# A post-norm decoder layer on one core: attention outputs turned by VectorE, and self attention's full-array products put ahead of its small ones

## The chip, the core and the metric

One core of a Trainium2 chip. Its engines are TensorE (PE, with a weight-load queue PEld), VectorE (DVE), ScalarE (ACT), GpSimd (POOL) and SyncE (SP, which here only issues DMAs). The metric is the device time of one execution in microseconds (us), as the median of several.

## What is computed

The input x has 8 batches of 512 tokens of width 256, and a context has 1024 tokens for each batch. Three sub-layers follow each other, each with the post-norm form x = layernorm(x + f(x)).

```
# self attention, 16 heads, key size 64, value size 16
scores = einsum(Q, K) / 8
Wmat   = scores * decay(t, s) * lam[level(t, s)]        # level: size class of t XOR s, 10 used
o      = einsum(Wmat, V) @ Wout.T + x;  layernorm(o) * ln_g + ln_b
# cross attention, 16 heads of size 16, 1024 keys
out    = softmax(q k / 4) v @ Wo.T + bo
# experts: 32 experts choose 8 tokens of each batch
probs  = softmax over tokens of (x @ gate_w.T + gate_b), then top_k(8)
merged = the chosen tokens weighted;  o = w2 gelu(w1 merged);  scatter-add o * vals
```

## The kernel before

The kernel is one program with three blocks, written out engine by engine. Every engine has its own instruction stream, and semaphores order the streams. In each stream the order is that of the code; nothing is scheduled by a tool. A block starts when every engine has left the one ahead of it.

**Self attention** (`self_attention`) runs through 8 batches of 8 head pairs, in sections `first`, `mid`, `last` and a `tail`. In iteration `i` TensorE works on three pairs at once: it projects queries and keys of pair i (`project_qk`, L468, 128x128 weights), makes the near scores of pair i-1 (`scores`, L501, tiles of 64x32) and its keys by token (`keys_by_token`, L490, transposes with 128x128 weights), and finishes pair i-2 (`states` L481, tiles of 128x64; `far` L516 and L522, tiles of 64x64; `near` L531, tiles of 32x32). PSUM results go through two lanes: `psA` with two slots, emptied by ScalarE, and `psV` with two slots, emptied by VectorE. `take_a` and `take_v` wait for the slot's last content to be gone. In the tail the first projections of cross attention run between the last pairs, and the layer norms of the last batch: GpSimd's `add_lnb` and `scale_by_lng` (L920, L914), VectorE's split of the projected keys in bf16 parts (`parts`, L183 to L192), whose rows the DMAs of `stack` (L200, L201) put into place.

**Cross attention** (`cross_attention`) first does 12 positions of maxima alone, and then 32 steps for each of 8 batches: 4 groups ("quads") of 4 heads, by 8 chunks of 128 keys. A step has the scores S of its chunk (L1459), four score products for the maxima of the step 12 ahead (`max_scores`, L1398), which VectorE reduces (L1680) from the three slots of `cpsV`, and the values product of the step before (`values`, L1420, four column tiles that add up in `acc`, called cacc in the trace). ScalarE takes the exponentials (L1586). Between these, at fixed steps, stand the jobs of the batch before (`prev`) and of the next one (`nxt`).

The path from `acc` to the output projection is what the change touches. After each quad ScalarE copies `acc` to `OT` (L1616); TensorE transposes it in four parts (`o_transposes`, L1439) in the step behind, ahead of the values product; VectorE divides by the sums (`outputs`, L1708, L1712) into O. When four quads are done TensorE transposes O in 8 parts (L1360 at step 2), ScalarE copies the result to oT (L1558), and at step 4 TensorE projects it (L1475) in four groups, each in a slot of `cpsV`. Later the gate's logits come from 4 recorded products with 32 columns of weights and 512 tokens (L1482, step 12), each streaming 512 columns; VectorE adds a bias (L1754), looks for the 8 largest and masks them; at step 20 the probabilities P8 are ready and SP saves them (L1319).

**SP's queue** issues in program order. In step 20 and behind it the order is: the save of P8, 12 DMAs of `stack_later(b + 1, 1)`, then `stack_max(b, 3)` (L1286), which moves the maxima nmT (12 KB) to where S of step 24 needs them. In the last batch weights of the experts are loaded by the same queue (`load_group_weights`, L1165, 1 MB each): 4 MB ahead of `stack_max(b, 3)`, and 8 MB at the end of the last step.

**Experts**: 8 groups of 4 experts, 8 MB of weights each group, loaded when the buffers come free; the loads of the fourth group's weights wait for the first group's first product and are issued after some small loads of SP.

Of the kernel before, what the change touches and what calls it, by code (L numbers as in the profile page):

```python
# [25 lines left out]
P = 128  # L26
# [5 lines left out]
G = T // P  # L32
# [103 lines left out]
OUTPUTS, X1T, PROJECT_V1, PROJECT_Q, MERGE, PROJECT_O, NORM = 1, 0, 1, 4, 2, 4, 7  # L136
PROJECT_K, X2T, COPY_X2, GATE, GATE_EXP, TOP8, TOP8_T, PICK, PICK_T = (7, 12), 9, 10, 12, 14, 20, 21, 28, 29
PROJECT_V0 = 20
# [173 lines left out]
def self_attention(nc, sh, dram):  # L312
    with ExitStack() as ctx:
# [103 lines left out]
        def _(pe):  # L417
            def body(sec, b):
# [194 lines left out]
                for i in range(PAIRS if now else 4):  # L613
# [13 lines left out]
                    if opening:  # L627
                        transpose_distances()
                        scored = take_v(("score", i))
# [7 lines left out]
                    if now:  # L637
                        project_qk(qk, 1, i)
                    if i == 2 and prev:
                        transpose_y()  # L640
                    if two is not None:
# [44 lines left out]
        def _(act):  # L686
            def body(sec, b):
# [71 lines left out]
                for i in range(PAIRS):  # L759
# [39 lines left out]
                    if sec == "tail" and i == 6:  # L799
# [3 lines left out]
                        nc.scalar.copy(ca.Vc[:, :, 0:8, 0:HD], full("cv").rearrange("p (c h d) -> p c h d", c=KT, d=HD)  # L803
# [7 lines left out]
        def _(pool):  # L811
# [19 lines left out]
            def body(sec, b):  # L831
# [69 lines left out]
                def layer_norm_factors(r):  # L901
                    pool.wait_ge(var, b * 2 + (r - 1))
# [38 lines left out]
                for i in range(PAIRS):  # L941
# [10 lines left out]
                    if i == 4 and prev:  # L952
                        add_lnb()
# [4 lines left out]
                    if i == 5 and prev:  # L958
                        scale_by_lng()
                    if i == 7 and prev:  # L960
                        layer_norm_factors(1)
                    if i == 1 and sec == "tail":
# [4 lines left out]
                        nc.gpsimd.memset(ca.Vc[:, :, :, HD:HD + 1], 1.0).then_inc(ca.vc_zeroed, 1)  # L967
# [7 lines left out]
        def _(dve):  # L975
# [3 lines left out]
            def body(sec, b):  # L979
# [117 lines left out]
                for i in range(PAIRS):  # L1097
# [37 lines left out]
                    if i == 6 and prev:  # L1135
                        dve.wait_ge(lnb_added, b)
                        dve.wait_ge(n1_scaled, b)
# [39 lines left out]
def ca_jobs(section):  # L1177
# [9 lines left out]
    for s in range(STEPS if now else TAIL_STEPS):  # L1187
# [3 lines left out]
        if prev:  # L1191
            a += {MERGE: ["oT"], X2T: ["x2T"]}.get(s, [])
# [6 lines left out]
        if s % KT == OUTPUTS and (now and s > KT or prev and s < KT):  # L1199
            v.append(("otr", (s // KT - 1) % QUADS))  # L1200
        if prev:
            v += [("wo", g) for g in range(G) if s == PROJECT_O]
# [921 lines left out]
```

## Time and profile before

| | us |
|---|---|
| median of 3 runs | 1839.48 |
| the three runs | 1838.58, 1839.82, 1839.48 |
| the profiled execution | 1839.74 |
| its span | 1837.9 |
| granted clock, mean over the span | 0.953 of full speed |

| stage | from, to (us of the span) |
|---|---|
| self attention, from the first products to its last pair | 22 to 594 |
| hand-over to cross attention | 594 to 629 |
| maxima alone | 629 to 660 |
| 8 x 32 steps of cross attention | 660 to 1646 |
| tail of cross attention for the last batch | 1646 to 1676 |
| experts, combine and store | 1676 to 1838 |

The profiled execution is 1.8 us longer than its span. Stage borders are read from the first and last instruction of each on TensorE. In rows of the timeline an entry merges equal instructions in a row; the distance from one row's start to the next one's is the time that the first took in the queue, which is less than its duration, since matmuls overlap at their ends. A matmul in float32 is recorded twice, a transpose once.

### The profile page before, as it was taken

The page shows a single profiled execution, that of the slowest core. Times are in us where ns is not written, and L with a number is a line of the kernel's source. Part 1 is how long each engine was busy: PE and PEld are TensorE (multiplying, and loading weights), DVE is VectorE, ACT ScalarE, POOL GpSimd, SP SyncE. Part 2 cuts the span into 40 slices and gives each one's busy share as a digit, 9 for nine tenths or more (in the row PEclk, how much of TensorE's full clock was granted, in tenths as well). Part 3 has the DMA queues.
Part 4 walks back from the last instruction along what each step waited for, and adds up shares of the span by engine and source line. Part 5 has one row for each costly group of instructions (what it writes and reads, how often), then busy time and mean ns, then how long its engine had stood idle before and what let it go on. Part 6 is the DMA issues. An engine that isn't in the chain of part 4 may idle for free. (4 is left out here: it accounts for less than half of the span.)

```text
span 1837.9 us, 48963 instructions
## 1 busy us (share of the span) xinstructions
PE 1678.5 (91%) x19924; PEld 806.8 (44%) x19924; DVE 1232.9 (67%) x2424; ACT 838.3 (46%) x1015; POOL 598.2 (33%) x970
## 2 busy tenths in 40 slices
PE   5999999999999699999999999999999999976564
PEld 3566666666665333343333433433433334223332
DVE  5767677677674777868778788788687787812005
ACT  2334344344333136655646565566556465651103
POOL 3545545645625536043043061250430420000002
PEclk8999999999999779999999999999999999987777
DMA  7000000000000221111202101112112024046995
GB/s 252 3 4 4 3 3 3 3 3 3 3 32 15 69 67 50 41 38 59 83 1 85 56 28 65 50 38 69 35 64 78 1 89 183 30 179 267 421 418 183
DMA packets 62205, 141.44 MB, mean 77 GB/s; under 512 B 11280, under 2 KB 34320, under 8 KB 54320
## 3 DMA queue, kind: packets, MB, share of 16 engines
q1 hardware_dynamic: 61520, 137.88, 20.6%
q8 instruction: 157, 2.57, 0.6%
q10 hardware_dynamic: 480, 0.59, 0.1%
q14 instruction: 48, 0.39, 0.1%
HBM read 92.43 MB, written 7.86 MB: 55 GB/s over the span
## 5 line engine op out<-in xcount | busy, mean ns | idle before, releaser
L1680 DVE TENSOR_REDUCE mx<-cpsV 128x1 f32<-128x512 f32 x1024 | 655.2, 686 | 187.5 <-PE cpsV L1398 175.3
L1586 ACT ACTIVATE w<-cpsA 128x1024 f32<-128x1024 f32 x512 | 496.3, 1021 | 246.0 <-PE cpsA L1459 240.8
L1398 PE MATMUL cpsV<-w 96*128 96x512 bf16 x1024 | 325.4, 394 | 21.6 <-DVEq L1663 13.0
L1459 PE MATMUL cpsA<-w 99*128 99x512 bf16 x1024 | 275.2, 382 | 22.4 <-DMA w<-nmT 10.1
L1420 PE MATMUL cacc<-w 128*32 128x512 f32 x2048 | 279.7, 607 | 0.4 <-ACT w L1586 0.4
L468 PE MATMUL psA<-w 128*128 128x512 f32 x512 | 257.0, 625 | 5.0 <-DVE WT L1102 1.8
L1398 PEld LDWEIGHTS cpsV<-w 96*128 96x128 bf16 x1024 | 86.1, 98 | 283.4 <-DVE mx L1680 197.0
L1648 POOL TENSOR_TENSOR crstd<-cmv,eps 128x4 f32<-128x4 f32 x8 | 1.6, 202 | 605.8 <-DVE cmv L1746 605.8
L765 ACT COPY w<-psA 128x1024 f32<-128x1024 f32 x64 | 64.8, 1012 | 229.3 <-PE psA L468 229.3
L1459 PEld LDWEIGHTS cpsA<-w 99*128 99x128 bf16 x1024 | 93.0, 98 | 163.0 <-ACT w L1564 15.8
L885 POOL TENSOR_TENSOR VP<-V,VPF 128x128 f32<-128x128 f32 (+2 forms) x256 | 129.2, 535 | 42.7 <-PE psA L481 36.8
L1111 DVE TENSOR_TENSOR tmp<-psV,CF 128x512 f32<-128x512 f32 x64 | 44.3, 692 | 121.7 <-PE psV L531 121.4
L468 PEld LDWEIGHTS psA<-w 128*128 128x128 f32 x512 | 87.9, 191 | 76.5 <-issue 67.7
L183 POOL TENSOR_TENSOR w<-w,zero 128x256 bf16<-128x256 f32 x88 | 51.1, 612 | 138.8 <-ACTq L1565 138.8
L1420 PEld LDWEIGHTS cacc<-w 128*32 128x32 f32 x2048 | 42.5, 108 | 92.5 <-issue 74.5
L2031 DVE TENSOR_TENSOR z<-psE,b1T 128x256 f32<-128x256 f32 x8 | 3.4, 424 | 110.5 <-PE psE L1967 110.5
L1981 PE MATMUL psE<-w,hT 128*32 128x256 f32 x512 | 39.6, 477 | 36.5 <-DMA w<-in_w 34.6
L1564 ACT COPY w<-cpsA 128x1024 f32<-128x1024 f32 x21 | 21.3, 1012 | 111.5 <-PE cpsA L1368 59.9
L1118 DVE TENSOR_REDUCE w<-tmp 128x128 f32<-128x512 f32 x64 | 67.8, 1059 | 4.7
L501 PEld LDWEIGHTS psV<-w 64*32 64x32 f32 x4096 | 41.2, 106 | 49.8 <-issue 48.1
L1385 PEld LDWEIGHTS cpsA<-w,w 128*128 128x128 f32 x480 | 54.7, 192 | 12.6 <-ACT w L1586 12.6
L192 POOL TENSOR_TENSOR w<-w 128x256 bf16<-128x256 f32 x88 | 57.1, 680 | 3.1
(224 smaller groups left out, 2227.6 us busy)
## 6 DMA issues: line engine op xcount, KB each, us to landing
w<-in_w SPq DMA_DIRECT2D x56, 1024.0 KB, 16.3
w<-w SPq DMA_DIRECT2D x189, 128.0 KB, 2.3
w<-w SPq DMA_DIRECT2D x189, 64.0 KB, 2.0
w<-in_ctxT SPq DMA_DIRECT2D x8, 1024.0 KB, 5.0
w<-in_xT SPq DMA_DIRECT2D x8, 512.0 KB, 6.4
x_tok<-in_x SPq DMA_DIRECT2D x8, 512.0 KB, 9.7
w<-in_w SPq DMA_DIRECT2D x8, 512.0 KB, 17.2
out_y<-w SPq DMA_DIRECT2D x16, 256.0 KB, 2.3
```

Source lines behind the costliest of these rows:

```text
L183: ops.tensor_tensor(cut(high, m), cut(r, m), zeros, ALU.add)
L192: ops.tensor_tensor(cut(low, m), cut(r, m), cut(mid, m), ALU.subtract)
L468: last = nc.tensor.matmul(out[:, n * T:(n + 1) * T], w[:, k, i * P:(i + 1) * P], XT[:, b, k, :], start=(k == 0), stop=(k == KD - 1))
L765: nc.scalar.copy(QK[:, i % 4, :], full(("qk", i))).then_inc(act_evac, 1)
L885: last = nc.gpsimd.tensor_tensor(VP[:, p % 2, g, 0:n, :].rearrange("q n (h c) -> q n h c", c=HD), vv.unsqueeze(1).broadcast_to([P, n, 2, HD]),
L1118: nc.vector.tensor_reduce(yp, tmp[:].rearrange("p g s c -> p g c s"), AX_X, ALU.add)
L1385: last = nc.tensor.matmul(out[:, c * P:(c + 1) * P], cT[:, k, c * P:(c + 1) * P], wv[:, k, hv * P:(hv + 1) * P], start=(k == 0), stop=(k = ...
L1398: nc.tensor.matmul(out, Qst[q // 2][0:ROWS, hh, g * P:(g + 1) * P], Kst[q // 2][0:ROWS, hh, half * BANK:(half + 1) * BANK], start=True, st ...
L1420: last = nc.tensor.matmul(acc[BLK * jj:BLK * (jj + 1), :], Vc[:, chunk, 4 * q + jj, :], Pr[:, (2 * s + jj // 2) % 4, (jj % 2) * T:(jj % 2 ...
L1459: last = nc.tensor.matmul(out[:, n * T:(n + 1) * T], Kst[q // 2][0:ROWS + 3, hh, chunk * P:(chunk + 1) * P], Qst[q // 2][0:ROWS + 3, hh, : ...
L1586: nc.scalar.activation(Pr[:, (2 * s + pp) % 4, :], src, ACT.Exp, scale=CA_SCALE).then_inc(act_evac, 1)
L1680: nc.vector.tensor_reduce(mx[:, q % 2, row, k % 2:k % 2 + 1], full(m[k]), AX_X, ALU.max).then_inc(dve_evac, 1)
```

## The change

Self attention: in an iteration TensorE now does queries, keys and keys by token in a row, and behind them scores, far and near. In the tail `add_lnb` is done ahead of the first norm's factors, and the product with ln_g by VectorE instead of GpSimd.

Cross attention: VectorE takes `acc` itself (`take_outputs`: a transpose in blocks of 32x32 from PSUM), divides, and transposes back (`outputs`); a DMA (`move_o`) puts 64 rows of each quad into oT. ScalarE's copy, both sets of TensorE's transposes and the copy to oT are gone. The values stand interleaved with zeros in Vc. The output projection has two groups of twice the width; the gate's logits come from column tiles, four token groups side by side, and four DMAs put them in one row block (`L4` to `L`), a step earlier than before; x2T goes in two jobs. In the tail `keep_clock` issues transposes of the identity that nothing reads.

```diff
@@ TensorE, self attention, iteration i
-                    if one is not None and not opening:
-                        scored = take_v(("score", i))
-                        evacuated_a(before(i, "qk"))
                     if now:
                         qk = take_a(("qk", i))
                         project_qk(qk, 0, i)
-                    if one is not None:
-                        scores(scored, one)
-                    if two is not None:
-                        out = take_v(("far", i))
-                        evacuated_a(("state", i))
-                    if now:
                         project_qk(qk, 1, i)
                     if i == 2 and prev:
                         transpose_y()
+                    if one is not None:
+                        evacuated_a(before(i, "qk"))
+                        keys_by_token(i, one)
+                        scores(take_v(("score", i)), one)
                     if two is not None:
+                        out = take_v(("far", i))
+                        evacuated_a(("state", i))
                         far(out, two)
...
-                    if one is not None:
-                        keys_by_token(i, one)
-                    if two is not None:
                         near(out, two)
@@ SP, cross attention
+            def move_o(bb, q):
+                sp.wait_ge(o_ready, bb * QUADS + q + 1)
+                sp.dma_start(oT[64 * (q % 2):64 * (q % 2) + 64, q // 2, :], byd[q % 2][0:P:2]
+                             ).then_inc(o_moved[q % 2], 16)
@@ TensorE, cross attention
-                    if s % KT == OUTPUTS and (now and s > KT or prev and s < KT):
-                        o_transposes(b if s > KT else b - 1, (s // KT - 1) % QUADS)
+                    if sec == "tail" and s == 1:
+                        pe.wait_ge(acc_evac, b * QUADS + 1)
+                        keep_clock(34)
                     if prev:
                         if s == PROJECT_O:
-                            evacuated_a("oT")
-                            for g in range(G):
-                                out = take_v(("wo", g))
...
+                            for of in o_moved:
+                                pe.wait_ge(of, b * 32 + 16)
+                            for r in range(2):
+                                out = take_v(("wo", r))
...
+                            keep_clock(28)
                         if s == GATE:
                             out = take_v("lg")
-                            evacuated_a("x2T")
+                            evacuated_a(("x2T", 1))
                             for k in range(KD):
-                                last = nc.tensor.matmul(out[0:E, :], gw[:, k, :], x2T[:, k, :],
-                                                        start=(k == 0), stop=(k == KD - 1))
+                                for g in range(G):
+                                    last = nc.tensor.matmul(out[E * g:E * (g + 1), 0:P], gw[:, k, :],
+                                                            x2T[:, k, g * P:(g + 1) * P], start=(k == 0), stop=(k == KD - 1))
                             last.then_inc(dve_full, 1)
+                            keep_clock(52)
...
-                    if prev and s == MERGE:
-                        pe.wait_ge(o_ready, b * QUADS)
-                        transpose_x("oT", O)
@@ VectorE, cross attention
+                def take_outputs(bb, q):
+                    dve.wait_ge(av_done, (bb * QUADS + q + 1) * KT)
+                    nc.vector.transpose(byq[q % 2][:].rearrange("p c s -> p (c s)"), acc[:]).then_inc(acc_evac, 1)
                     dve.drain()
+                def outputs(bb, q):
+                    t = byq[q % 2]
+                    nc.vector.reciprocal(rec[:], t[:, :, 1])
+                    dve.drain()
+                    nc.vector.tensor_tensor(t[:, :, 0:BLK:2], t[:, :, 0:BLK:2], rec[:].unsqueeze(2).broadcast_to([P, KT * 2, HD]),
+                                            ALU.mult)
+                    dve.drain()
+                    dve.wait_ge(o_moved[q % 2], bb * 32 + (q // 2 + 1) * 16)
+                    nc.vector.transpose(byd[q % 2][:], t[:].rearrange("p c s -> p (c s)")).then_inc(o_ready, 1)
+                    dve.drain()
...
+                    if now and s == TOP8:
+                        outputs(b, 1)
...
+                    if now and s and s % KT == 0:
+                        take_outputs(b, s // KT - 1)
+                    if prev and s == 0:
+                        take_outputs(b - 1, 3)
```

`outputs` stands at step 12 for quad 0 (behind a wait for the moved logits), at step 20 for quad 1 (behind P8), and at step 1 of the next batch for quads 2 and 3. In the last batch quad 2 is done at step 27.

TensorE in self attention, one iteration in the middle of a batch, first before and then after (psV and psA are the two lanes; w is a weight buffer):

```order
L481 MATMUL psA<-VP,Kt 64x48 x2
L468 MATMUL psA<-w_0 128x512 x2
L501 MATMUL psV<-w_1 32x32 x32
L468 MATMUL psA<-w_0 128x512 x2
L516 MATMUL psV<-Mst,w_1 64x64 x12
L516 MATMUL psV<-Mst,w_1 64x48 x4
L522 MATMUL psV<-Mst,w_1 64x16 x4
L490 MATMUL psA<-ident,w_1 128x128 x4
L531 MATMUL psV<-V,WT 32x16 x32
```

```order
L481 MATMUL psA<-VP,Kt 64x48 x2
L468 MATMUL psA<-w_0 128x512 x4
L490 MATMUL psA<-ident,w_1 128x128 x4
L501 MATMUL psV<-w_1 32x32 x32
L516 MATMUL psV<-Mst,w_1 64x64 x12
L516 MATMUL psV<-Mst,w_1 64x48 x4
L522 MATMUL psV<-Mst,w_1 64x16 x4
L531 MATMUL psV<-V,WT 32x16 x32
```

The three stretches with full 128x128 weights became one, and the three small products stand behind each other.

VectorE in cross attention around the end of a quad, before and after (mx<-cpsV are the maxima, 4 a step):

```order
L1680 TENSOR_REDUCE mx<-cpsV 128x1 x18
L1708 RECIPROCAL rec<-cpsV 128x16
L1712 TENSOR_TENSOR O<-cpsV,rec 128x64 x4
L1680 TENSOR_REDUCE mx<-cpsV 128x1 x10
L1685 TENSOR_REDUCE nm<-mx 128x16
```

```order
L1704 TENSOR_REDUCE mx<-cpsV 128x1 x16
L1732 STREAM_TRANSPOSE byq<-cacc 128x512
L1704 TENSOR_REDUCE mx<-cpsV 128x1 x12
L1709 TENSOR_REDUCE nm<-mx 128x16
```

The take now stands right behind the maxima of the quad's last step, two maxima sooner than the old division.

SP's queue at the end of cross attention, before and after (w_0 and w_1 from in_w are the experts' weights, byd is what `outputs` leaves):

```order
L1165 DMA w_0<-in_w 128x2048 x4
L1286 DMA w_1<-nmT 3x16x128
L1165 DMA w_1<-in_w 128x2048 x8
L1319 DMA p_scratch<-P 32x512
L1221 UNCONDITIONAL_BRANCH
```

```order
L1164 DMA w_0<-in_w 128x2048 x4
L1287 DMA w_1<-nmT 3x16x128
L1293 DMA oT<-byd 64x512
L1164 DMA w_1<-in_w 128x2048 x8
L1293 DMA oT<-byd 64x512
L1323 DMA L<-L 32x128 x4
L1339 DMA p_scratch<-P 32x512
L1218 UNCONDITIONAL_BRANCH
```

Behind the last eight loads of weights there is now a move of the last quad's outputs, and then the four of the logits.

## Rows read from the trace of the kernel before

**Rows 1.** Busy time by stage: PE, PEld, DVE, ACT, POOL, clock, DMA share, GB/s.

```profile
60.00:572.00 512.00, 507.16 (x12391) 328.09 (x12389) 349.94 (x640) 192.04 (x284) 259.58 (x418) 1.00 0.02 6
660.00:1644.00 984.00, 950.05 (x5264) 362.93 (x5262) 747.03 (x1509) 572.78 (x615) 244.94 (x398) 0.99 0.18 60
```

**Rows 2.** Timeline of TensorE, one pair: start, duration, line, operation, count.

```profile
304.16 0.76 PE L501 MATMUL psV<-w 64*32 64x32 f32 x64
304.85 1.98 PE L468 MATMUL psA<-w 128*128 128x512 f32 x4
306.76 0.68 PE L516 MATMUL psV<-Mst,w 64*64 64x64 f32 x32
...
307.46 0.66 PE L490 MATMUL psA<-ident,w 128*128 128x128 f32 x4
308.05 0.73 PE L531 MATMUL psV<-V,WT 32*32 32x16 f32 x64
308.79 0.79 PE L481 MATMUL psA<-VP,Kt 128*64 128x64 f32 x20
```

**Rows 3.** Timeline of the weight loads in the same pair.

```profile
302.78 0.19 PEld L468 LDWEIGHTS psA<-w 128*128 128x128 f32 x1 [0.24 <-issue]
303.21 0.19 PEld L468 LDWEIGHTS psA<-w 128*128 128x128 f32 x1 [0.24 <-issue]
```

**Rows 4.** Timeline, hand-over to cross attention.

```profile
610.03 1.22 DVE L183 TENSOR_TENSOR w<-w,zero 128x1024 bf16<-128x1024 f32 x1 [0.95 <-ACTq L746]
...
612.63 3.39 DVE L189 TENSOR_TENSOR w<-w,zero 128x1024 bf16<-128x1024 f32 x1
...
616.09 3.21 DVE L192 TENSOR_TENSOR w<-w 128x1024 bf16<-128x1024 f32 x1
```

**Rows 5.** Timeline of TensorE, steps 8 and 9 of a batch.

```profile
946.66 0.61 PE L1398 MATMUL cpsV<-w 96*128 96x512 bf16 x2
...
948.43 0.66 PE L1439 MATMUL cpsV<-ident,OT 128*128 128x128 f32 x4
949.02 1.06 PE L1420 MATMUL cacc<-w 128*32 128x512 f32 x8
950.01 1.09 PE L1522 MATMUL cpsA<-ident,o 128*128 128x128 f32 x8
950.94 0.60 PE L1398 MATMUL cpsV<-w 96*128 96x512 bf16 x2
```

**Rows 6.** Timeline of VectorE at the same place.

```profile
947.09 2.59 DVE L1680 TENSOR_REDUCE mx<-cpsV 128x1 f32<-128x512 f32 x4 [0.24 <-PE cpsV L1398]
```

**Rows 7.** Instructions of line L1047: count, ns (least, median, most).

```profile
L1047 DVE STREAM_TRANSPOSE w<-w x16: 1245/1245/1246, 52.2 to 545.3; 128x1024 f32<-128x1024 f32 x16
```

**Rows 8.** Timeline of TensorE, output projection at step 4.

```profile
923.52 2.86 PE L1475 MATMUL cpsV<-cwo,oT 128*128 128x256 f32 x12 [0.55 <-DVE mx L1680]
```

**Rows 9.** Timeline of SP and TensorE ahead of step 24.

```profile
874.08 0.77 SPq L1286 DMA_DIRECT2D w<-nmT  x1
...
876.33 1.04 PE L1459 MATMUL cpsA<-w 99*128 99x512 bf16 x4 [0.18 <-DMA w<-nmT]
```

**Rows 10.** The same step in the last batch.

```profile
1615.62 0.73 SPq L1286 DMA_DIRECT2D w<-nmT  x1
...
1625.11 1.89 PE L1459 MATMUL cpsA<-w 99*128 99x512 bf16 x4 [7.45 <-DMA w<-nmT]
```

**Rows 11.** Timeline of the tail: SP's weights, the projection, the next weights.

```profile
1643.21 4.27 SPq L1165 DMA_DIRECT2D w<-in_w  x8
...
1650.49 6.26 PE L1475 MATMUL cpsV<-cwo,oT 128*128 128x256 f32 x16 [1.10 <-ACT oT L1558]
...
1682.47 36.49 SPq L1165 DMA_DIRECT2D w<-in_w  x24
```

**Rows 12.** Stretches of the tail and of the experts, columns as in rows 1.

```profile
1660.00:1665.00 5.00, 3.27 (x10) 1.93 (x11) 1.36 (x4) 1.96 (x2) 0.00 (x0) 0.50 0.95 397
...
1677.00:1800.00 123.00, 84.33 (x928) 43.13 (x931) 3.82 (x9) 15.32 (x24) 2.54 (x9) 0.82 0.99 403
```

More of the change, by code:

```diff
@@ L901, in layer_norm_factors @@
                 def layer_norm_factors(r):
+                    if sec == "tail" and r == 0:
+                        pool.wait_ge(dve_evac, SA_DVE.count(sec, b, ("out", 1)) + DVE_SLOTS)
+                        add_lnb()
                     pool.wait_ge(var, b * 2 + (r - 1))
@@ L951, in body @@
                         level_logits()
-                    if i == 4 and prev:
+                    if i == 4 and prev and sec != "tail":
                         add_lnb()
@@ L1191, in ca_jobs @@
         if prev:
-            a += {MERGE: ["oT"], X2T: ["x2T"]}.get(s, [])
+            a += [("x2T", k) for k in range(KD) if s == X2T]
         if nxt:
@@ L1240, in cross_attention @@
         nmT = sb("nmT", [48, P], BF16)
-        OT = sb("OT", [P, T])
-        rec = sb("rec", [P, G, 4])
-        O = sb("O", [P, G, D])
+        byq = [sb(f"byq_{n}", [P, KT * 2, BLK]) for n in range(2)]
+        byd = [sb(f"byd_{n}", [P, T]) for n in range(2)]
+        rec = sb("rec", [P, KT * 2])
         o2 = sb("o2", [P, G, D])
@@ L1296, in body @@
                     stack_later(b, 3, free=CA_ACT.count(sec, b, ("s", 0, 1)) if prev else None)
+                if prev:
+                    if sec != "tail":
+                        move_o(b - 1, 2)
+                    move_o(b - 1, 3)
+                if now:
                     sp.wait_ge(act_full, CA_ACT.count(sec, b, ("v", 1)))
@@ L1433, in v0_evacuated, with keep_clock @@
                     return CA_ACT.start["mid"] + (b - 1) * CA_ACT.per_batch - back + 1 + 2
-                def o_transposes(bb, q):
-                    out = take_v(("otr", q))
-                    pe.wait_ge(acc_evac, bb * QUADS + q + 2)
-                    for g in range(G):
-                        last = nc.tensor.transpose(out[:, g * P:(g + 1) * P], OT[:, g * P:(g + 1) * P], sh.ident[:])
-                    last.then_inc(dve_full, 1)
+                def keep_clock(count):
+                    if sec == "tail":
+                        for _ in range(count):
+                            nc.tensor.transpose(acc[:, 0:P], sh.ident[:], sh.ident[:])
                 if sec == "pro":
@@ L1590, in body @@
                     if prev:
-                        if s == MERGE:
-                            to_rows("oT", oT)
                         if s == X2T:
-                            to_rows("x2T", x2T)
+                            for k in range(KD):
+                                nc.scalar.copy(x2T[:, k, :], full(("x2T", k))[:, 0:T]).then_inc(act_evac, 1)
                         if s == COPY_X2 and sec != "mid":
@@ L1611, in body @@
                             evac_v(0)
-                    if s % KT == 0 and ((now and s) or (prev and s == 0)):
-                        bb, q = (b, s // KT - 1) if s else (b - 1, 3)
-                        act.wait_ge(av_done, (bb * QUADS + q + 1) * KT)
-                        nc.scalar.copy(OT[:], acc[:]).then_inc(acc_evac, 1)
             sections(act, body)
@@ L1727, in body @@
                         max_jobs(s + LEAD, 0, 1)
-                    if s % KT == OUTPUTS and (now and s > KT or prev and s < KT):
-                        outputs((s // KT - 1) % QUADS)
+                    if prev and s == 1:
+                        if sec != "tail":
+                            outputs(b - 1, 2)
+                        outputs(b - 1, 3)
                     if prev:
@@ L1780, in body @@
                                                   ).then_inc(dve_evac, 1)
+                    if sec == "first" and s == GATE_MAX:
+                        outputs(b, 0)
+                    if now and s == TOP8:
+                        outputs(b, 1)
+                    if sec == "last" and s == LAST_OUTPUTS:
+                        outputs(b, 2)
                     if maxima:
```

126 lines of the change are left out of this document (71 added, 55 removed).

## The prediction

> **What bounds the kernel now.** I read the stretches by stage first, then the timeline of TensorE in each stage, then the waits where it stood idle. [rows 1] is the whole story of two thirds of the time: in self attention TensorE is busy for 507.16 of 512 us, in the steps of cross attention for 950.05 of 984, at full clock. VectorE follows with 747 of 984. So what counts is what stands in TensorE's queue, and what makes it stop. In the tail and the experts it is another matter: TensorE is half idle, and from 1677 to 1800 the DMAs are the bound, and the end moves with the moment at which the next weights are issued (rows in the part on the tail).
>
> **Self attention: three stretches of full weights become one.** [rows 2] is one pair in TensorE's queue, and [rows 3] gives the pace of a 128x512 product when nothing changes: two weight loads are 0.43 apart. Four of them, the keys, would take 1.72, but stand 306.76 - 304.85 = 1.91 in the queue: 0.19 is lost where small tiles follow. The queries lose as much ahead of the scores. The transposes by token take 308.05 - 307.46 = 0.59 for four; by [rows 5] eight take 950.94 - 950.01 = 0.93, so a transpose costs about 0.11 and four 0.43: 0.16 lost. Three such ends are 0.54, one is left: 0.38 a pair is gained. What comes in: scores ahead of far, and far ahead of near, two changes between small forms. The trace has one such change, near to states: 0.74 in the queue for 64 products with 0.63 of loads, 0.11. Two of them are 0.22. They replace two changes from small to full, of which 64 scores show one: 0.69 in the queue for the same loads, so 0.06 to 0.07; two are 0.14. Net 0.08 against: **0.30 a pair**, 62 pairs with all three parts, 18.6 us. Bounds: the new changes free, 0.52 a pair (32 us), or as dear as those after full products, 0.19 each, 0.14 a pair (9 us).
>
> Here a rule speaks: the Trainium skill, "TensorEngine Tiling (Array Packing)", section Key Properties, says that a change of tiling mode drains TensorE, and makes no difference between modes. An iteration had 7 changes and will have 5. At one price for all, 0.19 from [rows 2], two fewer give 0.38 a pair, 23.6 us and a total of 1819. The trace shows the changes to be unequal, dear after full products and cheap after small ones, so I stay with the sum by rows.
>
> New waits there: keys by token now need their slot of psA right behind Y's transposes (i = 2), while ScalarE still empties keys and queries (1.01 for 1024 columns, against 0.93 of transposes and some latency): 0.2 for 7 batches, 1.4 us. The other slots have more than an iteration's small products as cover (some 2.1 us), VectorE keeps its own distance: far's results are asked for 5.2 us after near has ended.
>
> **Hand-over: 4.2 us.** The split in parts takes 1.22 an operation when GpSimd is quiet, but 3.39 and 3.21 while it adds lnb and multiplies by lng [rows 4]. Everything to the start of cross attention hangs behind (copy, stacking DMAs, last norm). With add_lnb ahead and the product on VectorE behind the split, both fall to 1.22: 4.2 us.
>
> **Cross attention, quads.** Removed: four transposes ahead of the values, 949.02 - 948.43 = 0.59 each quad [rows 5]. Added: VectorE must have taken acc before the next values may start. The maxima of the quad's last step are issued at 946.66; VectorE works on them from 947.09, two in half of 2.59 [rows 6], to 948.39. A transpose of 128x1024 takes 1.245 [rows 7]; for 512 I estimate 0.7 (half is 0.62, a reduction of 512 from PSUM takes 0.65). So acc is free at 949.1, and TensorE, a semaphore later, starts the values at 949.18 instead of 948.43: it stands for 0.75. A quad loses 0.16 net; 31 quads, 5 us. The old division hid between maxima; the new one (reciprocal, product, transpose, about 1.6) stands at step 1 (twice), 12 and 20, where 3.5 us of V or K projection follow and leave VectorE idle. Without that cover it would cost its whole length.
>
> **Per batch.** O's eight transposes go, 0.93 [rows 5], and a wait for their copy, 0.24. The projection waits 0.55 and a little more for slots [rows 8]; with two slots wanted instead of four that is gone: 0.9. The gate's four products are streamed in 4 x 0.43 = 1.7 [rows 3]; four token groups side by side need a quarter, 0.45: 1.25 gained. x2T in two jobs: 0.15. Sum 3.45 a batch. The detour of the logits by DMA (issue four times 0.4, landing 2.2) is over when VectorE comes to it at step 12, about.
>
> **SP's queue.** At step 20 `move_o(b, 1)` comes ahead of the 12 stacking DMAs and waits until VectorE has done P8 *and* the outputs. The maxima's move lands 876.33 - 874.08 = 2.25 after issue, and S of step 24 waits for it already, 0.18 in this batch [rows 9]. It comes later by 1.6 for the outputs, plus the move's issue, less the save that used to run meanwhile: 1.75. Queued behind S on TensorE is all else. I take 1.65 for six middle batches, 9.9 us lost.
>
> Together: 7 batches x 3.45 = 24 would be gained, but in the last one what is gained ahead of step 8 only meets the maxima's move behind 8 MB of weights, and step 24 shifts by 1.75 [rows 10]: 6 x 3.45 = 20.7 and nothing for the last. 20.7 - 5 - 9.9 = **5.8 us** gained.
>
> **The tail: a loss.** Before, the last outputs reach the projection by ScalarE and TensorE at 1650.49 [rows 11]. Now they go by a DMA that SP issues at about 1648, behind eight loads of 1 MB. What a small transfer does behind large ones is in [rows 10]: 12 KB issued at 1615.62, behind 4 MB, landed at 1625.1, 9.5 instead of 2.25 later, and TensorE stood for 7.45. The 8.4 MB need 20 us at 0.42 MB a us; the stretch 1660 to 1665 is still 0.95 busy [rows 12]. So the projection starts at 1664.7, **14.2 us late**. `keep_clock(34)` fills 3.6 us of that and the rest is idle.
>
> Behind it things are faster. The granted clock there is 0.50 in 1660 to 1665 [rows 12], so products take double. The gate goes from 4 x 0.86 (twice the 0.43) to 0.5, the projection has one stall less, the copy of x2T overlaps, the fillers hold the clock for the small transposes; against that the logits' DMAs take 3.5. Step by step I come to P8T's end 2.7 earlier, counted from the projection. Net 11.5 us, and the reload of weights, and with it the end, moves by that: the next weights are issued at 1682.47 [rows 11], and from then to 1800 the DMA share is 0.99 [rows 12].
>
> A rule speaks against the fillers: the Trainium skill, "TensorE: Matmul & The Clock Gate", Part 4, has it that transposes don't count as work for the clock. By it the fillers do nothing, about 2 us more. No row of before shows whether transposes alone keep it up.
>
> **Sum**, against the profiled 1839.74: -18.6 + 1.4 - 4.2 - 5.8 + 11.5 = -15.7, so 1824.0; the median of the runs is 0.3 below the profiled one: **1823.8**.
>
> **Rivals.**
> *The small transfer overtakes the weights.* For it: a transfer is spread over 16 engines and is small. Against: [rows 10]. Then it lands 2.25 after 1648, at 1650.4, and the tail is 2.7 shorter instead of 11.5 longer: 1809.6.
> *Changes between small forms cost more than those after full products.* One mechanism, in TensorE's self attention. Each 0.01 of a change is 62 x 0.02 = 1.24 us. From 0.26 a change on the whole is slower (15 x 1.24 = 18.6 us away from the 0.11 taken); at 0.30 it is 24 more, 1847. For it: no row shows scores ahead of far, or far ahead of near, and the split of the array changes at each. Against it: near to states, 0.11.
> *VectorE becomes the bound in cross attention.* It is 76% busy in [rows 1] and gets 2.3 instead of 1.4 a quad; if the divisions aren't covered, 31 x 1.6 = 50 more, 1873; it loses all gain when 0.5 of each shows. For it: it idles only some 0.24 between two maxima. Against: the places, each in a projection's shadow.
> *The fillers don't hold the clock*: 1825.8, and nothing else changes.
>
> **Chances.** Forecast, with the fillers' case (a tenth) inside: 0.70. Overtaking 0.10. Small changes dear 0.12. VectorE bound 0.08. The forecast's own range comes from the bounds: small changes free or 0.19 each (-14, +10), take of acc 0.62 to 0.9 (-3, +6), SP's delay 0 to 1.75 a batch (-10, +1), tail by 3 each way. I give 1808 to 1841, which takes in the overtaking case. Under 0.2% (3.7 us) is no change that a measurement can tell. Faster 0.82, same 0.06, slower 0.12.
>
> **What would show it.** In the timeline after: in a pair, queries to the end of near 0.3 shorter, with no gap at far; S to values at a quad's end with TensorE waiting 0.75 for byq (L1732); S of step 24 waiting about 2 for nmT in the middle batches; a landing of the last move at 1645 + 19 on the old scale, with the projection waiting for it; the split's operations 1.22 each. Wrong: if the projection in the tail waits for VectorE and not for a DMA; if TensorE waits for a division; if the pair has the old length.

## The result and the profile after

| | us |
|---|---|
| before, median of 4 runs on the same chip | 1839.65 |
| after, median of 4 runs (1882.34 to 1888.22) | 1885.41 |
| ratio, with its 95% interval | 1.0249 (1.0231 to 1.0267) |
| forecast | 1823.8 |

The change made the kernel 46 us slower where 16 us of gain were forecast. Landmarks on TensorE, GpSimd and SP cut both spans into the same four pieces, which shows at once where to look:

| piece | before | after | difference | forecast |
|---|---|---|---|---|
| start to the first maxima (self attention and hand-over) | 628.89 | 658.16 | +29.3 | -21.4 |
| first maxima to the last values product | 1015.6 | 1015.7 | 0.0 | -5.8 |
| last values to the next weights issued by SP | 37.9 | 55.3 | +17.3 | +11.5 |
| from there to the end | 155.4 | 155.6 | +0.2 | 0 |

In the first piece the hand-over did as foretold. The split's operations in the timeline of VectorE, after, against [rows 4]:

```profile
643.43 1.23 DVE L183 TENSOR_TENSOR w<-w,zero 128x1024 bf16<-128x1024 f32 x1 [0.96 <-ACTq L737]
644.73 1.23 DVE L186 TENSOR_TENSOR w<-w 128x1024 f32<-128x1024 f32 x1
646.03 1.23 DVE L189 TENSOR_TENSOR w<-w,zero 128x1024 bf16<-128x1024 f32 x1
647.33 1.23 DVE L192 TENSOR_TENSOR w<-w 128x1024 bf16<-128x1024 f32 x1
```

So about 33 us were lost in self attention itself. A pair there, in the timeline of TensorE after, from states to states:

```profile
597.68 0.79 PE L481 MATMUL psA<-VP,Kt 128*64 128x64 f32 x20
598.39 3.70 PE L468 MATMUL psA<-w 128*128 128x512 f32 x8
601.93 0.60 PE L490 MATMUL psA<-ident,w 128*128 128x128 f32 x4
602.46 0.76 PE L501 MATMUL psV<-w 64*32 64x32 f32 x64
603.15 0.68 PE L516 MATMUL psV<-Mst,w 64*64 64x64 f32 x32
603.65 0.27 PE L522 MATMUL psV<-Mst,w 64*64 64x16 f32 x8
603.85 0.73 PE L531 MATMUL psV<-V,WT 32*32 32x16 f32 x64
604.51 0.79 PE L481 MATMUL psA<-VP,Kt 128*64 128x64 f32 x20
```

604.51 - 597.68 = 6.83. The old order took 7.26 (from 301.53 to 308.79, the end of which stands in [rows 2]): 0.43 gained, more than the 0.30 forecast. The scores still take 0.69 ahead of far (602.46 to 603.15), so the new changes between small forms are no dearer than I took them. But other pairs look like this:

```profile
301.20 0.76 PE L501 MATMUL psV<-w 64*32 64x32 f32 x64
301.88 0.68 PE L516 MATMUL psV<-Mst,w 64*64 64x64 f32 x32
302.39 0.27 PE L522 MATMUL psV<-Mst,w 64*64 64x16 f32 x8
302.59 0.63 PE L531 MATMUL psV<-V,WT 32*32 32x16 f32 x53
304.85 0.30 PE L531 MATMUL psV<-V,WT 32*32 32x16 f32 x11 [1.64 <-issue]
305.07 0.79 PE L481 MATMUL psA<-VP,Kt 128*64 128x64 f32 x20
305.79 5.40 PE L468 MATMUL psA<-w 128*128 128x512 f32 x8
```

Two things are to be seen. In the middle of near, after 53 of 64 products, TensorE stands for 1.64 and the trace knows no releaser ("issue"): no semaphore, no slot. Then the eight projection products take 5.40 instead of 3.70. The list of waits for the stretch 22 to 630 sums up the first (columns: waiting, releaser, total, times, longest):

```profile
PE psV L531 <- issue: 21.9, 15, 1.9
PE psA L481 <- issue: 7.7, 6, 1.9
```

With the lines L522 (2.3, twice), L516, L501 (1.3 each) and L452 (1.1) these are 26 pauses, 35.7 us; the old order had two, 1.7 us. (One more such wait in either list, ahead of the very first projection at 22 us, belongs to the start and is left out.) The stretches show the second, columns as in [rows 1]; the first line answers to the first line there:

```profile
60.00:572.00 512.00, 474.17 (x11463) 325.69 (x11462) 331.64 (x606) 177.41 (x266) 243.09 (x397) 0.96 0.02 6
302.00:304.00 2.00, 1.21 (x93) 1.10 (x94) 0.42 (x1) 2.00 (x5) 2.00 (x4) 1.00 0.03 8
304.00:306.00 2.00, 1.15 (x32) 1.07 (x32) 0.74 (x2) 0.42 (x2) 2.00 (x4) 1.00 0.00 0
306.00:308.00 2.00, 2.00 (x4) 0.72 (x4) 1.93 (x3) 0.27 (x1) 2.00 (x3) 0.61 0.03 8
308.00:310.00 2.00, 2.00 (x4) 0.89 (x3) 1.92 (x2) 0.00 (x0) 2.00 (x3) 0.54 0.00 0
```

The granted clock falls to its lower level (1.2 GHz) behind this pause, and comes back by 310. It does so behind about half of the 26, mostly the longer ones. 0.96 over 512 us at two levels means 8% of it at half speed, at most 20 us lost. As an estimate the account closes within 2 or 3: 34 more of pauses, 62 x 0.43 = 27 gained, 24 for the clock (20 and, at 0.95, 3 to 4 more from 572 to 640), 31 together against some 33.

**What the pauses are.** The one thing that moves in a pause is a DMA queue that no line issues. The DMA view of 302 to 303 has this one row (packets, MB):

```profile
q8 instruction: 1, 0.02, 6.5%
```

It is one packet of 16 KB. For the old order, 60 to 572, the same view says:

```profile
q8 instruction: 97, 1.59, 1.3%
```

[rows 1] has 12391 + 12389 records of products and weight loads there: 255.5 for each packet. So a packet is a block of 256 instructions of TensorE. Where the pauses lie says the same: if all records of TensorE in the trace are numbered in order of start, its weight loads and semaphore records among them, the first late record of each of the 26 has the same number but for a multiple of 256. Every pause stands on the border of a block, whatever product happens to be there. And each ends 2.2 to 2.8 us after the start of such a packet. Counting back from the pause above, 256 records before the first late one is a point 0.37 ahead of far, at 301.5: from the start of one block to the first instruction of the next it took 304.85 - 301.5 = **3.3 us** (3.5 if the semaphore records are counted with them). The theory to test: one block is fetched while the one before it runs, a fetch takes 3.3, and TensorE stands when 256 instructions pass in less. (3.3 is the figure of this one block and no constant. What holds for all 26 is the 2.2 to 2.8 from the packet: mostly the packet starts in the first 1.7 us of the block ahead. But eight blocks of this stretch passed in 1.6 to 2.0 without a pause in the list, and the packets behind them had started before they did, 2.4 to 4.2 ahead of the border; and three pauses, those that end at 204.29, 279.32 and 391.18, stand behind blocks of 6.7 to 8.9, in which the packet came only 4.3 to 6.6 after the start. What sets the moment of a packet isn't shown.) The new order has 188 products and 188 loads of small tiles in a row, 376 instructions in 2.7 us, 256 of them in 1.7. A block lies wholly inside the run in (376 - 256) / 256 of the pairs, 47% of 62, 29: 26 pauses were found, two of them in the last pair, behind the last projection.

The Trainium skill, "Runtime: NRT & Kernel Launch", section "Instruction fetch mechanics", has the blocks of 16 KiB and 256 instructions, and says that the fetch is hidden since instructions are issued more slowly than blocks come. The trace agrees on the block and differs on the hiding.

Rival theories: (B) changes between small forms cost, now and then a lot; (C) the clock falls by itself, and pauses follow from it. Against B speaks already the place of the pauses, on the borders of blocks and not at changes of form: the one above stands in the middle of near. Against C speak the stretches above: the clock is still 1.00 from 302 to 306, in which the pause lies, and falls behind it.

### The profile page after: what moved, and what is told of

It is laid out like the page before. It is cut to its first block and busy times, and to the rows that moved or that the text cites. A ratio compares the mean times of both kernels' runs of the same rounds, so it can differ in the third digit from the quotient of the medians.

```text
span 1884.7 us, 48947 instructions
## 1 busy us (share of the span) xinstructions
PE 1664.0 (88%) x19958; PEld 825.0 (44%) x19958; DVE 1266.6 (67%) x2377; ACT 811.4 (43%) x983; POOL 590.5 (31%) x969
## 5 line engine op out<-in xcount | busy, mean ns | idle before, releaser
L1420 PE MATMUL cpsV<-w 96*128 96x512 bf16 x1024 | 327.9, 395 | 22.1 <-DVE mx L1704 13.0
L468 PE MATMUL psA<-w 128*128 128x512 f32 x512 | 252.5, 638 | 3.6 <-issue 3.2
L468 PEld LDWEIGHTS psA<-w 128*128 128x128 f32 x512 | 97.6, 201 | 110.1 <-issue 105.5
L1096 DVE TENSOR_TENSOR WT<-psV,w 128x256 f32<-128x256 f32 x64 | 27.0, 422 | 102.6 <-PE psV L501 99.9
L2026 PE MATMUL psE<-w,hT 128*32 128x256 f32 x512 | 38.2, 464 | 37.9 <-DMA w<-in_w 36.0
L531 PE MATMUL psV<-V,WT 32*32 32x16 f32 x4096 | 50.1, 181 | 22.1 <-issue 21.9
L481 PE MATMUL psA<-VP,Kt 128*64 128x64 f32 (+2 forms) x1280 | 53.8, 228 | 11.9 <-issue 7.7
```

The lines of the kernel that those rows point to most:

```text
L468: last = nc.tensor.matmul(out[:, n * T:(n + 1) * T], w[:, k, i * P:(i + 1) * P], XT[:, b, k, :], start=(k == 0), stop=(k == KD - 1))
L481: last = nc.tensor.matmul(out[r, HD * slot:HD * (slot + count)], Kt[:, g * P + S * hh:g * P + S * hh + S], VP[:, p % 2, g, column:column + ...
L1420: nc.tensor.matmul(out, Qst[q // 2][0:ROWS, hh, g * P:(g + 1) * P], Kst[q // 2][0:ROWS, hh, half * BANK:(half + 1) * BANK], start=True, st ...
L2026: last = nc.tensor.matmul(psO[m][BLK * j:BLK * (j + 1), :], hT[:, c, j, :], w2[m][j][:, c, :], start=(c == 0), stop=(c == FC - 1))
```

## The experiments

**1. The old order with the rest of the change.** The self attention part of the diff is undone.

> The change without its self attention part: the old order there, all else as changed. Every theory of the stalls says the same here: 26 pauses of TensorE for which the trace names no releaser are gone, the clock stays at 1.0 from 69 to 600, and what is left is the hand-over (-4.4), cross attention (+1) and the tail (+17.3), so 1839.65 + 13.9 = 1853.5, within 3. If it comes out near 1885, the self attention order is not the cause; near 1840, order and tail hang together in a way I have not seen.

Measured: 1853.09 (1849.08 to 1858.91), ratio 1.0077 (1.0058 to 1.0095). The clock from 60 to 572 is 1.00, two pauses in self attention, first maxima at 625.96, 2.9 ahead of before. So the order costs 32, all else 15. Single executions of this kernel differ by up to 10 us, with a granted clock of 0.950 to 0.956 over the whole, so medians are compared, and single traces only for what a wait or a pair shows.

**2. Small products in two runs.**

```
scores(one); far(two)              # ahead of the key projection
project_qk(1); keys_by_token(one)  # then full weights
near(two); states(next)
```

> Small products in two runs instead of one: queries, scores, far, keys, keys by token, near, states. Theory A (instruction supply: 256 instructions are fetched as a block, and a pause comes when 256 of them pass in less than the 3.3 us that a fetch takes): every 256 instructions hold at least one projection of 1.85 us and take 3.6 or more, so no pauses, clock at 1.0, and one costly change from full to small tiles less than in the old order, some 0.2 a pair, 12 us: 1841. Theory B (changes between small forms are what costs): scores to far is one of the two new changes, so about half of the 33 us: 1870. Theory C (the granted clock falls by itself and the pauses follow): no reason why it should differ from the full change, about 1885.

Measured: 1859.86, ratio 1.0118 (1.0101 to 1.0135). The pauses are gone but for two (0.82, on the border of a block, and 0.54, which isn't), and the clock is 1.00, as theory A says and B doesn't. But the time was missed by 19 us: it is 7 more than with the old order. Keys by token come later against near, and so does their copy, for which the next states wait. The list of waits has a new first line:

```profile
PE psA L481 <- ACT Kt L766: 16.4, 33, 0.5
```

**3. Keys by token between far and near**, all else as in the change.

> As the full change, but the four transposes of keys by token stand between far and near. Theory A: 256 instructions across the transposes take at least 2.3 us instead of 1.7, still under 3.3: as many pauses as before (20 to 30), but of about 1.0 us instead of 1.4 to 1.9; 26 x 0.5 = 13 less of pauses, against 0.16 a pair, 10 us, lost at the end of the transposes: about 1880. Theory B: only one new change between small forms, scores to far, as in the two-run kernel: about 1870 and no pauses. Theory C: 1885.

Measured: 1864.74, ratio 1.0152 (1.0134 to 1.017). 20 pauses in self attention, 20.9 us in sum. In the timeline of TensorE:

```profile
290.09 0.66 PE L490 MATMUL psA<-ident,w 128*128 128x128 f32 x4
290.68 0.63 PE L531 MATMUL psV<-V,WT 32*32 32x16 f32 x53
292.26 0.30 PE L531 MATMUL psV<-V,WT 32*32 32x16 f32 x11 [0.96 <-issue]
```

At the same product of the run as above it stands for 0.96 instead of 1.64: four transposes, 0.59, shorten the pause by 0.68. Theory B has no place for that. The clock is 0.99 over 60 to 572: it fell behind 4 of the 20 pauses, so short ones cost less of it. The time is 15 less than I gave: 20 pauses instead of 26, and less loss of clock.

**4. More small products, no new change of form.** Old order, the 32 score products issued three times (the same values again).

```
for _ in range(3):
    for g in range(G):
        ...
```

> Old order, but each pair's 32 score products are issued three times (the same values again, so the result is unchanged): a run of 384 small instructions of one form, and no new kind of change between tiles. Instruction supply: 256 of them pass in 1.4, a fetch takes 3.3; the two ends of a block fall inside the run in (384 - 256) of some 656 instructions, 1 iteration in 5: 10 to 15 pauses without a releaser, of 1.5 to 1.9 each, inside the scores or just behind them; time 1853 + 64 x 2 x 0.69 + 15 to 25 = 1955 to 1970. If the pauses came from changes between small forms: none, 1941.

One run: 2030.74. 55 pauses in self attention (60 to 770), 76 us in sum, against two, in an order that has no new kind of change:

```profile
316.48 1.55 PE L502 MATMUL psV<-w 64*32 64x32 f32 x161
319.89 0.36 PE L502 MATMUL psV<-w 64*32 64x32 f32 x31 [1.85 <-issue]
```

This settles A against B: no change of form was added, and the pauses came, again all on the borders of blocks. The clock, 1.00 in the old order, is 0.97 over 60 to 572. The number of pauses was missed: I divided by the length of an iteration, where a block starts every 256 instructions, two or three times in one of 656. 31 of the pauses are of 1.4 to 2.7; the others are shorter, as they should be for blocks that hold some products of the projection.

**5. Keys by token right behind the keys**, ahead of far; the longest run of small products is 248 instructions.

```
project_qk(1); keys_by_token(one)
far(two); near(two); states(next)
```

> Old order but for one thing: keys by token stand right behind the key projection, ahead of far, so that two stretches of full weights are left instead of three, and the longest run of small products is 248 instructions. Instruction supply: a window of 256 nearly always holds full products (3.6 us or more); at most 3 short pauses. One costly change less, 0.12 a pair as a pair of the two-run kernel showed (7.15 against 7.27); and the copy of the keys by token comes ahead of far, so states don't wait for it as they did there: 62 x 0.12 = 7.5 less than the old order alone, 1845.5. If tile changes all cost alike: 62 x 0.19 = 12 less, 1841. If states still wait 0.5 in half of the iterations: 1853 to 1860.

Measured: 1842.25, ratio 1.0025 (1.0015 to 1.0034); 10.8 less than experiment 1. One pause (2.45, at the end of the last batch, where no projection is left). The pair in the timeline of TensorE:

```profile
342.63 0.79 PE L481 MATMUL psA<-VP,Kt 128*64 128x64 f32 x20
343.35 1.98 PE L468 MATMUL psA<-w 128*128 128x512 f32 x4
345.27 0.76 PE L501 MATMUL psV<-w 64*32 64x32 f32 x64
345.95 1.98 PE L468 MATMUL psA<-w 128*128 128x512 f32 x4
347.77 0.60 PE L490 MATMUL psA<-ident,w 128*128 128x128 f32 x4
348.30 0.68 PE L516 MATMUL psV<-Mst,w 64*64 64x64 f32 x32
348.81 0.27 PE L522 MATMUL psV<-Mst,w 64*64 64x16 f32 x8
349.01 0.72 PE L531 MATMUL psV<-V,WT 32*32 32x16 f32 x64
349.66 0.79 PE L481 MATMUL psA<-VP,Kt 128*64 128x64 f32 x20
```

7.03 against 7.26: 0.23 gained, twice what I took from experiment 2. Against [rows 2] the keys take 1.82 instead of 1.91, the transposes 0.53 instead of 0.59, and near 0.65 instead of 0.74, since it follows small tiles now. The first maxima start at 613.78, 12.2 earlier.

**6. The tail: the last move first.** Old order; SP issues the last `move_o` ahead of the last eight loads.

> Old order in self attention, and SP issues the last move of outputs ahead of the last eight loads of weights. Queue theory (a small transfer waits behind the 8 MB issued ahead of it on its queue): the projection starts 5 to 6 us after the last values instead of 22, some 16 earlier; against that the logits' four transfers are now behind the 8 MB, so the top-8 waits some 4 longer: 12 us less than with the old order alone, 1841. Rival (VectorE's take, division and transpose are what the projection waits for, or the experts' weights set the end anyway): within 3 of the old order alone, 1851 to 1854.

Measured: 1844.16, ratio 1.004 (1.0027 to 1.0053), 8.9 less than experiment 1. The timeline of after, and then of this kernel, around the projection:

```profile
1672.50 4.51 SPq L1164 DMA_DIRECT2D w<-in_w  x8
1673.82 1.06 PE L1442 MATMUL cacc<-w 128*32 128x512 f32 x8 [0.36 <-ACT w L1613]
...
1677.34 0.48 SPq L1293 DMA_DIRECT2D oT<-byd  x1
...
1695.88 4.40 PE L1499 MATMUL cpsV<-cwo,oT 128*128 128x256 f32 x12 [16.22 <-issue]
```

```profile
1635.40 1.06 PE L1452 MATMUL cacc<-w 128*32 128x512 f32 x8 [0.36 <-ACT w L1623]
...
1641.53 3.69 PE L1509 MATMUL cpsV<-cwo,oT 128*128 128x256 f32 x16 [0.30 <-issue]
...
1667.32 1.12 PE L1527 MATMUL cpsV<-ident,P 128*128 128x128 f32 x4 [9.12 <-DVE P L1815]
```

The projection starts 6.1 after the last values instead of 22.1 (the trace calls the wait "issue", but the move, issued at 1677.34, landed 18.5 later, at 1695.8, just ahead of the first product; here it landed 2.5 after issue). The logits' moves are now the small ones behind 8 MB: they land 9.3 after issue instead of 2.2, and TensorE waits 9.12 for P8, where it was 1.91.

**7. The small moves on another queue.** ScalarE issues the last move and the logits' four.

> Old order in self attention; the last move of outputs and the four moves of the logits are issued by ScalarE, on its own DMA queue, and SP's eight loads keep their place. Theory: what makes the small transfer late is its place behind the loads in SP's queue. Then it lands 2 to 4 us after issue although 8 MB are under way, the projection starts 6 to 8 us after the last values instead of 21.6, and the logits don't wait either: 1853.1 (old order alone) less 15 to 18, about 1836. Rival: the 16 engines are full and serve what came first whatever the queue; then the projection starts 18 to 22 after the last values and the time is that of the old order alone, 1853.

Measured: 1845.76, ratio 1.0046 (1.0029 to 1.0063). The answer is between the two:

```profile
1652.88 0.54 ACTq L1617 DMA_DIRECT2D oT<-byd  x1
...
1660.68 5.94 PE L1508 MATMUL cpsV<-cwo,oT 128*128 128x256 f32 x16 [5.49 <-issue]
```

7.8 from issue to use (landed after 7.7), against 18.5 in the queue behind the weights, and 2.6 in the kernel of experiment 11 with none of the last weights ahead (1611.85 to 1614.46). Another queue lets a small transfer by; the busy engines still delay it by 5.

**8. The same without any fillers** (`keep_clock` issues nothing).

> As the kernel with the small transfers on ScalarE's queue, without any of the unread transposes in the tail. If transposes hold the clock, the gate, the transposes of P8 and the small products behind them run at half clock and the step from projection to the next weights is 2 to 4 us longer. If they don't count, the clock rows are the same, and since the last ten fillers stand 1.9 us ahead of the end of the block, the time is about 2 us shorter.

Measured: 1844.66, ratio 1.005 (1.0028 to 1.0072): no difference in time that can be told. But in the stretch of the gate, first with fillers and then without (there the gate comes 8 us earlier):

```profile
1670.00:1675.00 5.00, 4.16 (x42) 3.28 (x43) 1.73 (x5) 2.02 (x3) 0.09 (x1) 1.00 0.11 44
```

```profile
1662.00:1667.00 5.00, 3.23 (x24) 2.05 (x24) 1.12 (x4) 2.12 (x3) 0.00 (x0) 0.50 0.05 20
```

The fillers, transposes all, do hold the full clock (2.4 GHz) through the gate, whose products take 0.64 with them and 1.08 without. P8's transposes, behind a wait, take 0.66 and 1.11 in these two traces, but 1.07 in that of the change, which has the fillers too: so the fillers don't hold the clock that far every time. What they win, 1.0 up to P8, is lost again by the last ten, which stand ahead of the block's end (6.2 from P8's transposes to the next block's first work against 4.8).

**9. SP's queue in the batches.** Old order; `move_o(b, 1)` behind `stack_max(b, 3)`.

> Old order in self attention; SP's move of quad 1 stands behind the twelve stacking transfers and the maxima's move instead of ahead of them. Theory: the wait for the outputs ahead of the maxima's move is what makes S of step 24 wait 0.8 to 1.9 in each batch; it falls to what before.py had (0 to 1.1), so 6 to 8 us less than the old order alone: 1846. Rival: the outputs are ready before the saved P8 is issued and only the move's own issue, 0.55, counts: 4 us less in all batches, or nothing, 1849 to 1853.

Measured: 1842.36, ratio 1.0031 (1.0018 to 1.0045), 10.7 less than experiment 1, more than I had expected. The wait of S for the maxima's move, first in the kernel of experiment 1 and then here:

```profile
PE cpsA L1489 <- DMA w<-nmT: 19.8, 9, 9.4
```

```profile
PE cpsA L1489 <- DMA w<-nmT: 11.0, 4, 8.9
```

Between the two traces this wait accounts for 8.8.

**10. What helped, together**: the order of experiment 5, SP's order of 9, in the tail the last move, four loads, the logits' moves, the save of P8, four loads, and without the last ten fillers.

> What helped, together: keys by token behind the keys (10.8 less than the old order alone), SP's move of quad 1 behind the maxima's move (10.7 less), and in the tail the last move ahead of the first four loads, the logits' moves behind these four and the other four loads behind the save of P8, without the last ten fillers. Theory: the tail was held up only by small transfers behind large ones. Then from the last values to the next weights it takes about 36 instead of 56, so 1853.1 - 10.8 - 10.7 - 20 = 1812, faster than before.py by about 1.4%. Rival: the four loads that are put off collide with the experts' own and push the end, or the gains share a cover: 1820 to 1830.

Measured: 1818.92, ratio 0.99 (0.9884 to 0.9915). The tail is 35.1 as expected; from the next weights to the end it takes 162.9 instead of 155.5: the rival has a third of the gain. It is small transfers behind large ones once more. The experts' first small loads (b1r, b) are now issued behind the four that were put off and land 9 to 10 after issue, where it was 2 to 3, and TensorE waits for them, 3.37 and 2.68:

```profile
1660.30 1.08 PE L2011 MATMUL psE<-ident,b1r 32*128 32x32 f32 x8 [3.37 <-DMA b1r<-in_w]
```

**11. And in the last batch the maxima's move ahead of 4 MB of weights.**

> As the one before, and in the last batch the maxima's move stands ahead of 4 MB of weights instead of behind them. Queue theory: the wait of 9 at step 24 of the last batch falls to under 1, 7 to 8 less than the kernel before it: about 1804. Rival: the DMAs are the bound at the end and the 4 MB that come 10 later push the experts: no gain.

Measured: 1807.92 (1806.63 to 1808.45), ratio 0.9841 (0.9828 to 0.9855). The wait of 8 to 9 is gone from the list, the stretch from maxima to last values is 993.8, and this version is 1.6% faster than before, 4% faster than the change as it was (0.9841 against 1.0249).

## Why the prediction was wrong

**Self attention, the failed step.** "Net 0.08 against: 0.30 a pair" priced each product by the rate at which its kind ran in the old order, and took TensorE's queue as something that always holds the next instruction. The changes of form were right in sign, and their gain even too small (0.43 in a pair without a pause). The term put at nothing was instruction supply: small products are the cheapest in time and the dearest in instructions, 376 of some 400 in a pair, and the full products between them, which I counted as a cost for their changes of mode, were the time in which the next block arrived. Pauses 34 and the clock that fell behind them 24, an estimate from its mean, stood against the 27 gained. In none of my rivals was this mechanism; "small changes dear" gave the right side for a reason that the rows refute: the changes taken at 0.11 each cost nothing that shows (scores 0.69 ahead of far, far 0.70 ahead of near, as in the old order), which is why the pair gained more than forecast. Within the pair the rule that I had weighed and left did better than my sum: with two changes of tiling fewer 0.43 was gained, with one fewer (experiment 5) 0.23, so one price of some 0.22 for each fits both sums. The Trainium skill, "TensorEngine Tiling (Array Packing)", Key Properties, states that a change drains TensorE, and gives no price; two sums don't make one a rule, and row by row 0.28 of the 0.43 lies in queries and keys.

**The slot wait at i = 2**, 1.4 forecast: 2.5 in 7 times in the list of waits. Right, a little small.

**Hand-over**, 4.2: from the last pair's work to the first maxima 34.8 became 30.5 (594.07 to 628.89, 627.71 to 658.16). Right. With the old order the gain was 2.9.

**Cross attention**, 5.8 forecast, nothing found. By the starts of the values products seven batches took 866.0 instead of 869.9, and the last one 112.9 instead of 107.7: 3.9 gained and 5.1 lost (1.0 was gained ahead of the first).

The term of the quads was right in sign and reason. A quad was to lose 0.16, 5 in all; its end, in the timeline of TensorE after, with [rows 5] against it:

```profile
973.57 0.60 PE L1420 MATMUL cpsV<-w 96*128 96x512 bf16 x2
974.75 1.07 PE L1442 MATMUL cacc<-w 128*32 128x512 f32 x8 [0.58 <-DVE byq L1732]
```

1.18 from the maxima to the values, where it was 949.02 - 947.97 = 1.05 with the transposes between: 0.13 lost here, and 1.9 in the sum of 30 quads, since some hide it.

The 3.45 a batch were too much. Where products were taken out at steps 2 and 12, the values behind them now wait for ScalarE's exponentials, which was hidden before (0.77 here, 9.3 in 16 times, 1.2 a batch):

```profile
935.31 1.06 PE L1442 MATMUL cacc<-w 128*32 128x512 f32 x8 [0.77 <-ACT w L1613]
```

SP's queue cost about what was forecast: step 24 waits 0.4 to 1.9 for nmT in the batches ahead of the last, 7.4 in sum against 1.9 before, and experiment 9 gave 10.7 back where 9.9 was the term. The last batch, which I had at nothing, is the largest miss, 5.1: the wait behind 4 MB grew from 7.45 to 9.7 and an earlier one for nmT from 0.7 to 2.1, and the clock was at 0.67 in the stretch 1590 to 1600.

**Tail**, 11.5 forecast, 17.3 found. The mechanism is the one predicted, small behind large: the projection starts 16.1 later against 14.2. The 2.7 to be won behind it weren't there: up to P8's transposes 0.6 was gained, and from there to the next weights 1.8 lost, where the last fillers stand (33.2 against 32.0 in all). The overtaking rival was wrong on one queue, and half right on two.

**VectorE as the bound**: no wait for a division anywhere in the list. But TensorE's waits for slots of the maxima, which VectorE empties, grew from 5.9 (21 times) to 13.0 (36 times), while 3.8 of such waits at the projection went; whether the takes and divisions are behind it wasn't tested. **Fillers**: they hold the clock through the gate, against the Trainium skill, "TensorE: Matmul & The Clock Gate", Part 4; that the total didn't move was right for another reason.

Still open is why 2.2 to 2.8 us pass from the start of a packet to the end of a pause, what sets the moment of a packet, and whether a run of small products can be made without the pauses by having fewer instructions; nothing of this was tried.

## What to carry to other kernels

Count instructions, not only time: where 256 instructions of TensorE passed in less than about 3.3 us here, the next ones mostly waited for their own code, so spread long products between runs of small ones, and treat an "issue" wait in mid-run that ends some 2.5 us behind a packet of the instruction queue as that. A product taken out of a queue was also somebody's cover; ask what waits behind it. And a small transfer that the path needs is issued ahead of the megabytes, not behind them: 18.5 us against 2.6 here.

## What the hardware showed unexpectedly

- Instruction blocks of 16 KB, one for each 255.5 records of TensorE. All 26 pauses of the change, the 20 of experiment 3 and the 55 of experiment 4 stand on borders of blocks; those of the change end 2.2 to 2.8 us after the start of a packet (1.64 behind 256 instructions in 1.7; in experiment 3 0.96 with four transposes among them, in experiment 4 1.85 in a run of one form).
- The granted clock fell to the lower level after single pauses of 1.6 us in an engine that was otherwise full, though not after each, and cost by estimate 24 us beside 34 of pauses; pauses of about 1.0 cost little (0.99 against 0.96).
- Transposes that nothing reads kept the clock at its upper level around the gate of the tail: 1.00 against 0.50 without them.
- One change of tile form fewer in a pair gave 0.23 (experiment 5), two fewer 0.43 (the change), in a pair without a pause.
- A small transfer behind large ones on one queue landed with them: 128 KB 18.5 us after issue behind 8 MB, 7.7 on another engine's queue, 2.5 ahead of them.
